# A scatter that starts behind a shorter clearing, with its padding rows cleared afterwards, in a four-layer graph network on one Trainium2 core

## The reference

```python
edge_index = jnp.stack([src, dst])
h = jnp.maximum(_layernorm(x), 0.0)
x = x + L0(h, edge_attr_64, ...)   # messages: leaky([h[dst], ea] @ w1 + b1) @ w2 + b2, summed by src; then an update net
h = jnp.maximum(_layernorm(x), 0.0)
x = x + L1(h, W, attn, rel, ...)   # attention over edges, weights by softmax over dst, scaled by rel[etype]
h = jnp.maximum(_layernorm(x), 0.0)
x = x + L2(h, ...)                 # graph convolution, norms from degrees, mish
h = jnp.maximum(_layernorm(x), 0.0)
x = x + L3(h, ...)                 # mean over neighbours, two products, relu
```

## Time and profile before

| | us |
|---|---|
| median of 3 executions | 3375.53 (3375.49 to 3376.52) |
| profiled execution | 3380.8 |
| its span, first to last instruction | 3379.1 |
| PE, DVE, ACT, POOL busy | 2511.1, 2597.0, 1489.4, 1952.3 |

### The profile page before, as it was taken

One profiled execution on the slowest core, in us unless ns is written; L12 is line 12 of the kernel. 1 busy time (PEld: TensorE's weight loads), 2 busy tenths in 40 slices (PEclk: granted clock), 3 DMA queues, 4 the chain that ended last, 5 costly groups with the idle time before them and its releaser, 6 DMA issues. The chain is left out here.

```text
span 3379.1 us, 87741 instructions
## 1 busy us (share of the span) xinstructions
PE 2511.1 (74%) x20390; PEld 1974.6 (58%) x20391; DVE 2597.0 (77%) x8325; ACT 1489.4 (44%) x3942; POOL 1952.3 (58%) x2344
## 2 busy tenths in 40 slices
PE   1433555555555554999999999999999239989899
PEld 1322334333334343999999999999997214445455
DVE  7863777777777773999999999999997779983501
ACT  2011222222222222677777777777775655452200
POOL 1005777777777777899999999999996000000000
PEclk9975677677777776999999999999999559999999
DMA  9993222222222223888888888888886669869766
GB/s 381 414 414 129 78 78 83 78 78 78 77 79 78 78 68 104 236 240 234 242 239 235 240 239 234 242 238 236 241 239 226 255 282 343 301 219 315 249 220 208
DMA packets 738172, 696.84 MB, mean 206 GB/s; under 512 B 48524, under 2 KB 637275, under 8 KB 734779
## 3 DMA queue, kind: packets, MB, share of 16 engines
q1 hardware_dynamic: 516770, 536.77, 47.6%
q10 hardware_dynamic: 195544, 104.71, 12.7%
q0 software_dynamic: 25792, 54.52, 4.9%
HBM read 340.91 MB, written 354.90 MB: 206 GB/s over the span
## 5 line engine op out<-in xcount | busy, mean ns | idle before, releaser
L855 POOL DMA_INDIRECT sorted_rows<-rows,posi x806 | 785.1, 974 | 338.7 <-issue 221.4
L1147 DVE SCALAR_TENSOR_TENSOR acc<-acc,keep,pm 128x256 f32<-128x256 f32 x1504 | 715.7, 476 | 70.9 <-issue 23.9
L965 POOL TENSOR_SCALAR ohs_e<-iota,rt 128x128 f32<-128x128 f32 x1128 | 666.2, 607 | 12.4 <-DMA rt<-sorted_rows 12.4
L803 PE MATMUL s_peq<-sb_w1bb,eT 128*128 128x256 f32 x806 | 352.5, 531 | 398.9 <-ACT eT L658 379.9
L1074 PE MATMUL pm<-ohw_e,ohs_e 128*128 128x128 f32 x3008 | 609.1, 283 | 0.0
L974 POOL TENSOR_TENSOR hid<-pre_e,excess 128x512 f32<-128x512 f32 x376 | 482.8, 1284 | 117.2 <-ACT excess L1001 117.2
L1080 PE MATMUL px<-PN,dT 128*128 x4512 | 498.1, 219 | 0.4 <-ACT dT L1014 0.4
L1020 ACT ACTIVATE ohw_e<-ohd_e,rt 128x128 f32<-128x128 bf16 x1504 | 490.5, 397 | 0.0
L1074 PEld LDWEIGHTS pm<-ohw_e,ohs_e 128*128 128x128 f32 x3008 | 461.8, 194 | 0.0
L803 PEld LDWEIGHTS s_peq<-sb_w1bb,eT 128*128 128x128 f32 x806 | 172.8, 265 | 441.1 <-ACT eT L658 432.7
L1091 PE MATMUL ps<-hid,ohs_e 128*128 128x129 f32 x3008 | 424.3, 283 | 0.5 <-POOL hid L974 0.5
(11 more groups left out here) (317 smaller groups left out, 4206.3 us busy)
## 6 DMA issues: line engine op xcount, KB each, us to landing
count_matrices<-acc SPq DMA_DIRECT2D x1504, 128.0 KB, 2.6
sorted_rows<-zrow SPq DMA_DIRECT2D x188, 528.0 KB, 10.5
rt<-sorted_rows ACTq DMA_DIRECT2D x184, 528.0 KB, 4.6
gab<-count_matrices SPq DMA_DIRECT2D x60, 1280.0 KB, 6.0
arb<-count_matrices SPq DMA_DIRECT2D x25, 1664.0 KB, 8.8
ab<-count_matrices SPq DMA_DIRECT2D x25, 1600.0 KB, 9.3
arb<-count_matrices SPq DMA_DIRECT2D x25, 1536.0 KB, 8.5
ef<-in_edge_attr_dram SPq DMA_DIRECT2D x58, 364.0 KB
```

Of the source, the lines that this page charges most:

```text
L803: nc.tensor.matmul(pe_q[:, q % 2, 0:2 * D], eT[:, q % 2, :], w1bb[:], start=True, stop=True).then_inc(s_q, 1)
L855: pool.indirect_dma_start(sortd, bass.IndirectOffsetOnAxis(ap=posi[:, h, c:c + 1], axis=0), rows[:, h, c, :], None).then_inc(s_sc[h], 16)
L965: last = nc.gpsimd.tensor_scalar(ohs[:, k % BUFS, j, :], iota128[:], rt[:, k, j, D + 1:D + 2], None, ALU.is_equal)
L1147: nc.vector.scalar_tensor_tensor(acc[:, k % SUMS, j, :], before, keep[:, at:at + 1] if isinstance(at, int) else keep[:, ds(at, 1)], pm[:, ...
```

## The change

- **Blind clearing** covers only tiles EDGE = 1000 to 1503 (63 transfers instead of 188). It is issued by SP, behind the loads of indices, weights and biases, which all move to SP; ACT issues only the nodes.
- **Exact clearing** of the rows below tile 1000 that no edge fills follows the scatter on POOL, as indirect transfers from a longer `zrow` (64 rows for each partition, copied on ACT). The padding of a bin is cut into strips of 64 (twice, where needed), 32, 16, 8, 4, 2 and 1 rows by the bits of its length: eight indices for each bin, in five lots of 125 bins, so 40 transfers. Two more clear whole tiles at the end of a src group, four the free tiles behind the last group. Indices that name nothing lie beyond the bound and are skipped. In the edge stage SP waits for the first ten of these transfers before it loads, ACT for the other 36 before its fourth round.
- **One-hots** in the front come from f16 inputs with the column as the innermost dimension, 52 columns at a time; HT copies and small weight products move to ACT.
- **Table search** moves from the front into seven bodies of the scatter on DVE, between `places(i, 0)` and `begin(i, 1)`. The search numbers tiles along partitions, so it needs no transposes. `keep` and `tilei` are loaded at the end of the scatter.
- **Projections** `PN` move from the front to the end of the second block, behind its last edge projection; ACT writes the first and second part, DVE the rests.
- Buffers are laid over others that are not in use (`raw`, `ef` and `junkW` in `tile_tables`, one-hots in `S`, others in `H`), so POOL's two fills of `ef` and `rows` shrink to one of a single word for each row; the first positions stand ahead of the next `begin`.

```diff
+PADS = ((192, 64, 1), (128, 64, 2), (32, 32, 0), (16, 16, 0), (8, 8, 0), (4, 4, 0), (2, 2, 0), (1, 1, 0))
+EDGE = 1000
+FREE = 100
+PADP = 125
+BEYOND = 1048576.0
...
-                    for k, a in enumerate((dst, src, et)):
+                    for k, a in enumerate((src, dst, et)):
+                        row = (1, 0, 2)[k]
...
-                    sp.wait_ge(s_z, 2)
-                    with sp.Fori(0, CLEARED) as n:
-                        sp.dma_start(zv[ds(n, 1)].squeeze(0), zrow[:].rearrange("p k w -> p (k w)")).then_inc(s_zd, 16)
...
+                    for name, fr in (("bs", bs), ("bn", bn)):
+                        sp.dma_start(brow[name][:], fr.rearrange("(a d) -> a d", a=1)).then_inc(s_ld, 16)
+                    sp.dma_start(c1col[:], c1.rearrange("(d a) -> d a", a=1)).then_inc(s_ld, 16)
+                    sp.dma_start(b2col[:], b2.rearrange("(d a) -> d a", a=1)).then_inc(s_ld, 16)
+                    sp.dma_start(c2bc[:], c2.partition_broadcast(P)).then_inc(s_ld, 16)
+                    sp.dma_start(b1bc[:], b1.partition_broadcast(P)).then_inc(s_ld, 16)
...
+                    sp.wait_ge(s_z, 2)
+                    sp.wait_ge(s_xl, 32)
+                    sp.wait_ge(s_ix, 16 * 9)
+                    with sp.Fori(BLIND, TT // ZR) as n:
+                        sp.dma_start(zv[ds(n, 1)].squeeze(0), zrow[:, 0:ZR, :].rearrange("p k w -> p (k w)")).then_inc(s_zd, 16)
+
+                @block.scalar
+                def _(act):
+                    act.wait_ge(s_pd, 1)
+                    act.dma_start(X[:, 0:NT - 1, :], x[0:(NT - 1) * P, :].rearrange("(t p) d -> p t d", p=P)).then_inc(s_xl, 16)
+                    act.dma_start(X[0:NR, NT - 1, :], x[(NT - 1) * P:N, :]).then_inc(s_xl, 16)
+                    act.wait_ge(s_z, 2)
+                    for k in range(1, PADS[0][1] // ZR):
+                        nc.scalar.activation(zrow[:, k * ZR:(k + 1) * ZR, :], zrow[:, 0:ZR, :], ACT.Copy)
...
+                    act.wait_ge(s_dv, 4)
+                    act.dma_start(padr.rearrange("k (s d) -> s k d", s=NT), pout[:]).then_inc(s_st, 16)
+                    act.dma_start(fullr, fout[:]).then_inc(s_st, 16)
...
-                        nc.vector.tensor_tensor(ohs[:, n % 2, 0:w, :], iota32[:].unsqueeze(1).to_broadcast([P, w, QP]),
-                                                tile[:, 1, c].unsqueeze(2).to_broadcast([P, w, QP]), ALU.is_equal)
-                        nc.vector.tensor_tensor(ohd[:, n % 2, 0:w, :], iota25[:].unsqueeze(1).to_broadcast([P, w, NT]),
-                                                tile[:, 0, c].unsqueeze(2).to_broadcast([P, w, NT]),
+                        nc.vector.tensor_tensor(ohs[:, n % 2, :, 0:w], rep32[:, :, 0:w],
+                                                tile[:, 1, c].unsqueeze(1).to_broadcast([P, QP, w]), ALU.is_equal)
+                        nc.vector.tensor_tensor(ohd[:, n % 2, :, 0:w], rep25[:, :, 0:w],
...
+                    link(nc.vector.tensor_tensor(pbit[:], npad[:].unsqueeze(1).to_broadcast([NT, NPB, NT]),
+                                                 pmask[:].unsqueeze(2).to_broadcast([NT, NPB, NT]), ALU.bitwise_and))
+                    nc.vector.tensor_scalar(cnt[:, 7, 4:5], cnt[:, 6, NT - 1:NT], 2.0, None, ALU.mult)
+                    nc.vector.tensor_scalar(pidx[:, 1, :, :], pbit[:, 0:len(PADS), :], 0.0, BEYOND, ALU.is_equal, ALU.mult)
+                    for k, (bits, size, back_) in enumerate(PADS):
+                        if back_:
+                            nc.vector.tensor_scalar(pidx[:, 0, k, :], cnt[:, 0, :], float(back_), None, ALU.subtract)
+                        else:
+                            last = nc.vector.tensor_scalar(part[:, k - 2, :], pbit[:, len(PADS) + k - 2, :], 1.0 / size, None, ALU.mult)
+                    link(last)
+                    for k, (bits, size, back_) in enumerate(PADS):
+                        if not back_:
+                            last = nc.vector.scalar_tensor_tensor(pidx[:, 0, k, :], cnt[:, 0, :], float(P // 2 // size), part[:, k - 2, :],
+                                                                  ALU.mult, ALU.subtract)
+                    link(last)
+                    nc.vector.tensor_tensor(pout[:], pidx[:, 0, :, :], pidx[:, 1, :, :], ALU.add)
+
+                    link(nc.vector.tensor_scalar(fidx[:, 0, :], six[:], cnt[:, 7, 3:4], None, ALU.add))
+                    link(nc.vector.tensor_scalar(fidx[:, 1, :], fidx[:, 0, :], cnt[:, 7, 4:5], BEYOND, ALU.is_ge, ALU.mult))
+                    nc.vector.tensor_tensor(fout[:], fidx[:, 0, :], fidx[:, 1, :], ALU.add).then_inc(s_dv, 1)
...
+                    act.wait_ge(s_st, 48)
+                    with nc.allow_non_contiguous_dma(reason="bins in order of partitions"):
+                        act.dma_start(padi[:], padr.rearrange("k (c p) -> p k c", p=PADP)).then_inc(s_pi, 16)
+                        act.dma_start(fulli[:], fullr.rearrange("s (j c) -> (s j) c", c=2)).then_inc(s_pi, 16)
+                    act.dma_start(incb[:], rowinc.partition_broadcast(P)).then_inc(s_pi, 16)
+                    act.wait_ge(s_pad, 1)
...
+                    act.wait_ge(s_ts, 1)
+                    act.dma_start(tilef.rearrange("(p j) -> p j", j=TCOL), tilk[:]).then_inc(s_to, 16)
+                    act.dma_start(tiler.rearrange("k (p j) -> p k j", j=TCOL), tili[:, 0:3, :]).then_inc(s_to, 16)
                     step(BODIES - 1, False, True)
+                    act.wait_ge(s_to, 32)
+                    act.wait_ge(s_te, BODIES * PAIRS)
+                    act.wait_ge(s_pos, 2 * BODIES)
+                    act.dma_start(keep[:], tilef[0:TT].partition_broadcast(P)).then_inc(s_tl, 16)
+                    for k in range(3):
+                        act.dma_start(tilei[:, k, :], tiler[k:k + 1, 0:TT]).then_inc(s_tl, 16)
                     projected(BODIES - 1, PAIRS - 1)
+                    for g in range(NQ + 1):
...
+                    def tables(part):
+                        link = link_t
+                        if part == 0:
+                            dve.wait_ge(s_pi, 48)
+                            nc.vector.scalar_tensor_tensor(freei[:], incb[0:FREE, BINS - 1:BINS].to_broadcast([FREE, 4]), 2.0, four[:],
+                                                           ALU.mult, ALU.add)
+                        if part < PIECES - 1:
+                            w = 3 * TCOL // (PIECES - 1)
+                            for n in range(part * w, part * w + w):
+                                k, j = n // TCOL, n % TCOL
+                                ins = nc.vector.tensor_scalar(junk4[:, j % 4, :], incb[:], kidx[:, k, j:j + 1], None, ALU.is_le,
+                                                              ALU.add, accum_out=table[:, k, j:j + 1])
+                                if j % 4 == 3:
+                                    link(ins)
+                            return
...
-                    with dve.Fori(2, BODIES) as i:
+                    for i in range(2, 2 + PIECES):
+                        begin(i, 0, False)
+                        positions(i - 1, 1, False)
+                        places(i, 0)
+                        tables(i - 2)
+                        begin(i, 1, False)
+                        positions(i, 0, False)
+                        places(i, 1)
+                    with dve.Fori(2 + PIECES, BODIES) as i:
...
+                    pe.wait_ge(s_cq, BODIES * PAIRS)
+                    for g in range(NQ):
+                        if g >= 2:
+                            pe.wait_ge(s_pp, first_rest[g - 2])
+                        for t in range(4 * g, min(4 * g + 4, NT)):
+                            o = (t % 4) * P
+                            nc.tensor.matmul(pe_q[:, g % 2, o:o + D], HT[:, t * P:(t + 1) * P], wl["w1a"][:], start=True, stop=False)
+                            last = nc.tensor.matmul(pe_q[:, g % 2, o:o + D], ones[0:1, :], b1bc[0:1, :], start=False, stop=True)
+                        last.then_inc(s_pn, 1)
...
-                    nc.gpsimd.memset(ef[:], 0.0).then_inc(s_pad, 1)
-                    nc.gpsimd.memset(rows[:], 0.0).then_inc(s_pad, 1)
-                    pool.wait_ge(s_zd, 16 * (TT // ZR))
+                    nc.gpsimd.memset(rows[:, :, :, D + 3:D + 4], 0.0).then_inc(s_pad, 1)
+                    pool.wait_ge(s_zd, 16 * (TT // ZR - BLIND))
+
+                    def clear(index, parts, size, done):
+                        spots = sortd.rearrange("(n s) w -> n (s w)", s=size)
+                        pool.indirect_dma_start(
+                            spots, bass.IndirectOffsetOnAxis(ap=index, axis=0),
+                            zrow[0:parts, 0:size, :].rearrange("p k w -> p (k w)"), None,
+                            bounds_check=EDGE * P // size - 1, oob_is_err=False).then_inc(done, 16)
...
+                    pool.wait_ge(s_pi, 48)
+                    pool.wait_ge(s_ts, 1)
+                    for c in range(2):
```

(79 more changed lines are left out.)

349 lines of the change are left out of this document (173 added, 176 removed).

## The result

The changed kernel takes 3397.05 us (median of 13, 3385.52 to 3425.18), the kernel before 3376.57 (3374.46 to 3379.78): ratio 1.0077, 95% interval 1.0054 to 1.01. It is **slower by 0.8%**; 3288 had been forecast, and the range to 3340 misses it.

The account below looks back on a forecast made before the run. The path was taken as clears, 806 scatter issues on POOL, edge stage, layers. From the profiled 3380.8, minus 168 (start) plus 18 (DVE's lead) plus 62 (strips) gave 3292.8, as a median 3288 us; range 3260 to 3340.

Parts of the forecast that it names:

- Start: Before the scatter: fewer blind clears let POOL's first scatter start at 112 us instead of 280.19; gain 168, bounds 179 and 143.
- 8 us credited to a queue that runs ahead of its landings: SP's clears: the last issue precedes the landings, so it was put at 92 us instead of 100.
- new load ahead of its first copy: ACT, after the first block's barrier: loading the pad indices, 5000 single words, costs up to 5 us more.
- DVE's lead: Scatter: POOL starts on the first finished half while DVE also searches tables, so POOL stalls; loss 18 us, bounds 4 and 34.
- Rival A: Scatter: DVE becomes the bound of the whole scatter, losing 53 us instead of 18; 3323 us, chance 0.12.
- Strips: POOL behind the scatter: 46 more indirect transfers at 1.28 us, bytes nearly in step; loss 62 us, bounds 44 and 90.
- half more than the mean on the busiest: Strips' bytes: upper bound if the DMA engines share them unevenly, 90 us.
- Its block can't end before: Scatter block's end: it comes only after POOL has issued the 46 added transfers, 59 us.
- moved projections: PE at the scatter's end: 36 us for 25 tiles, longer at a lower granted clock, covered by 59 us of strips.
- Rival B: Strips use few DMA engines, 5 of 16, and run into the edge stage; 3375 us, no change, chance 0.07.
- C: POOL behind the scatter: the strips' issue grows with their bytes; loses from 3.3 us an issue, up to 3577; chance 0.10.
- D: Before the scatter: the start moves only to 160 us, held by single words or DVE's chain; 3336 us, chance 0.03.

Follow-up runs that it names:

- experiment 6: Changed kernel with 128-wide strips at the end, index tables' loads moved from ACT's queue to SP's: 3304.13 us, 0.9782 of the kernel before.
- experiment 5: Changed kernel, strips moved ahead: 42, 125 wide, before the scatter 3378.93 us; all 46, 128 wide, tables on SP's queue, 3289.53; these behind 26 scatters 3290.23.
- experiment 2: Changed kernel with strips of 128, 126 or 127 bins instead of 125, last lot shorter and filled up: 3318.58, 3344.4 and 3967.65 us.
- experiment 4: Changed kernel, scatter block ending without waiting for POOL's transfers, tables in memory not reused: 3378.46 us; with 128-wide strips 3310.19.
- experiment 3: Changed kernel with all 188 clears blind on SP: without strips 3408.5 us; with strips whose places all lie out of bounds 3474.33.
- the three dead places: Changed kernel, each strip issued over 128 places instead of 125, the last three always out of bounds: 3315.66 us, 0.9812 of the kernel before.

## Why the prediction was wrong

- **Start, 168 us forecast, 151.7 measured, within the bounds.** SP's last clear was issued at 98.9 instead of 92: 1.30 us each, but the 8 us credited to a queue that runs ahead of its landings did not come. The "new load ahead of its first copy", put at "up to 5 us more", was the right place and half the size: the three loads take 9.9 us (experiment 6). DVE's front ended at 81.4 (86 forecast), so SP covers it, as said. Its 1.7 us for 52 columns of one-hots does not follow from the rows it cites (4.1 us x 52/65 x 421/681 is 2.0); 1.9 was measured.
- **DVE's lead, 18 us forecast, 10.9 measured, cause half wrong.** It was put down to a stall behind a thin lead. The traces account for all of it: the gaps between scatters are 7.2 us longer in sum than before (250.0 against 242.8, added up along POOL's timeline), 5.9 of them ahead of seven scatters between 231 and 414 us, in bodies 3 to 8, where DVE also searches the tables, as the prediction's signs had it; and the scatter instructions 3.7 us longer, 3.3 of them in a single one of 4.25 us near the end (at 1134.5; the longest before takes 1.35), which every rebuilt kernel has and for which no run shows a cause. But 59 us of strips ahead bring back only 4, and 0.7 of that in the gaps (experiment 5). Rival A is dead: it priced this loss at 53.
- **Strips, 62 us forecast, 185 measured (in the slowest execution): the step that failed.** Its issue term was sound: 46 at 1.28 is what a 128-wide strip costs (1.0 and 0.3), 68 in all for 125 wide. What failed is the step that moves their bytes "At 404 GB/s", so that "some 3 us may stick out into the edge stage": that is the rate of transfers of 128 pieces, and was put on transfers of 125, which moved 221 GB/s at first and 33 at the end, with 107 us behind the last issue. The upper bound for uneven engines, "half more than the mean on the busiest", was far too small: it is 193 us from the first strip to the edge stage, against a mean of 57 of work for each engine (an estimate: 22.1 + 2.6 MB at the 27 GB/s of experiment 2 on each of 16).
- **The block's end.** "Its block can't end before" was said of the issues, and of the waits "nothing". The end also stands behind the landing of every strip (experiment 4), so all of the drain is on the path. The moved projections were hidden, as forecast: over at 1177, under the strips. That they take "longer at a lower granted clock" did not come: 1.45 us a tile at a granted clock of 0.50 (1.2 GHz; 1150 to 1170 us), as at 1.00 (2.4 GHz) in the front of the kernel before.
- **Rival B had the mechanism,** at 0.07, and with the wrong place: it let the strips run into the edge stage, 3375 us. With the block's end open 3378 comes out, but that they agree is partly luck: B reckoned with the same five engines throughout, where 88% of the engines' time is used at first, and with a stage that shares the DMA engines from its start, where its first rows come 37 us behind its start instead of 6. "Against: the scatters and clears, of 128 partitions, show no sign of it" was no argument, as they could not show it: the indirect transfers of the kernel before all have 128 places.
- **Rivals C and D.** C is dead: a strip is issued in 1.19 us, far from 3.3, and takes as long when it moves no bytes (experiment 3). D asked for a start at 160; it was 128.
- **With the three dead places the sum nearly closes:** 3315.7 against 3288, of which 17 are the start, 15 the strips' drain (85.6 from scatter to edge stage, less 8.2, against 62) and -7 the scatter; 3 are left open.

## What to carry to other kernels

Give an indirect transfer of large pieces 128 places, even if places that write nothing fill it up: 125 and 128 places differ by 81 us here, and 127 cost 571 more than 125. That any multiple of 16 would do was not tried. Before putting work behind the last instruction of a block, ask what its end waits for: here not only for POOL's issue but for every landing. Look for a place where the landing lies under other work; the issue stays on POOL. And loads of index tables in single words belong on a queue behind which nobody waits.

## What the runs showed of the hardware that was not expected

The issue of a strip on POOL follows neither its places nor its bytes: 0.98 us for 128 places, 0.99 for 126, 1.19 for 125, 2.54 for 127 (and 0.99 for the strips of 100 places in each of them). The packets of its queue rise in the same order, at equal bytes. The queue's rows in the whole profile (packets, MB, share) with 128, 125 and 127 places:

```profile
q0 software_dynamic: 31088, 79.25, 6.9%
```

```profile
q0 software_dynamic: 39248, 79.29, 7.7%
```

```profile
q0 software_dynamic: 87088, 79.55, 6.8%
```

Empty strips of 125 places have the same 39248 packets and land within 2.8 us, so the packets alone are not what drains late. The same 25 MB need 84 us from last scatter to edge stage or over 700. The times of single executions spread by 31 to 40 us in the three kernels whose strips of 125 places move bytes (10 to 13 executions each), and by 1 to 12 us in all others (4 or 5 each), the one with 127 places among them (5 us); why only 125 spreads so far is open.
